# A four-layer graph network on one core: who evicts the first attention layer's products, and who sums the second layer's rows

## What is computed

```python
def _gat_conv(x, W, att_src, att_dst, b, src, dst):
    h = (x @ W).reshape(n, HEADS, HID)                     # 4 heads of 64
    a_s = jnp.einsum('nhc,hc->nh', h, att_src)
    a_d = jnp.einsum('nhc,hc->nh', h, att_dst)
    e = jax.nn.leaky_relu(a_s[src] + a_d[dst], NEG_SLOPE)
    m = jax.ops.segment_max(e, dst, num_segments=n)
    ex = jnp.exp(e - m[dst])
    denom = jax.ops.segment_sum(ex, dst, num_segments=n)
    alpha = ex / denom[dst]
    msg = h[src] * alpha[:, :, None]
    return jax.ops.segment_sum(msg, dst, num_segments=n).reshape(n, HEADS * HID) + b
...
h = jax.nn.elu(_gat_conv(x, W1, att_src1, att_dst1, b1, src, dst))   # src, dst with self-loops
h = jax.nn.elu(_gat_conv(h, W2, att_src2, att_dst2, b2, src, dst))
...
x = _layernorm(x + h)
```

## Time and profile before

| | us |
|---|---|
| median of 3 runs | 7264.87 (7262.79 to 7265.74) |
| the profiled execution | 7259.0 |
| its span | 7257.3 |
| first attention layer, 2860 to 3552 of the span | 692 |
| second attention layer, 3552 to 4400 | 848 |
| graph convolution layer, 4400 to 4872 | 472 |
| third attention layer, 5533 to 6330 | 797 |
| last attention layer, 6330 to 7257 | 927 |

### The profile page before, as it was taken

How to read it: one execution, slowest core, us unless ns; L and a number is a source line. 1 busy time by engine, 2 the same in 40 slices (tenths; PEclk the granted TensorE clock), 3 DMA queues, 4 the chain that set the end, 5 groups by cost and what they waited for, 6 DMA issues and landing times. The chain is left out here.

```text
span 7257.3 us, 77301 instructions
## 1 busy us (share of the span) xinstructions
PE 3818.6 (53%) x18205; PEld 3002.3 (41%) x18205; DVE 4910.7 (68%) x15616; ACT 3204.3 (44%) x7082; POOL 3988.0 (55%) x3216
## 2 busy tenths in 40 slices
PE   3578880088866884777400005988884666700000
PEld 1267760077755663555400003547773555600000
DVE  6544555545548875999698886866666888676664
ACT  0023330033324552444255555758884777633333
POOL 4767776667766877342244425621114444178887
PEclk9689995599998997999755557999997888855555
DMA  8745447845448996676577767989995666476665
GB/s 307 273 92 77 77 64 272 328 69 78 77 56 318 350 348 212 234 245 235 186 260 260 249 244 286 380 302 327 334 336 188 215 219 211 163 265 226 226 227 188
DMA packets 646102, 1633.93 MB, mean 225 GB/s; under 512 B 128454, under 2 KB 283878, under 8 KB 630290
## 3 DMA queue, kind: packets, MB, share of 16 engines
q1 hardware_dynamic: 459954, 1234.83, 48.9%
q0 software_dynamic: 185696, 394.18, 20.3%
HBM read 816.50 MB, written 813.62 MB: 225 GB/s over the span
## 5 line engine op out<-in xcount | busy, mean ns | idle before, releaser
L1708 PE MATMUL l_pb<-l_jx,k_ones 128*128 128x128 f32 x26 | 6.1, 399 | 1595.9 <-DVE l_jx L1941 1595.9
L802 POOL DMA_INDIRECT NS<-e_tot,e_idx x392 | 647.9, 1653 | 283.3 <-ACT e_tot L1060 210.8
L2244 ACT ACTIVATE l_z<-l_a,l_nb,l_rs 128x256 f32<-128x256 f32 x1176 | 609.7, 598 | 392.7 <-DMA out_dram<-l_z,k_ids 389.9
L1667 POOL DMA_INDIRECT l_eg<-HBT,k_nsrc x392 | 508.2, 1296 | 384.8 <-DVEq L1886 145.0
L1708 PEld LDWEIGHTS l_pb<-l_jx,k_ones 128*128 128x128 f32 x26 | 5.0, 284 | 1596.6 <-DVE l_jx L1941 1596.6
L936 DVE TENSOR_SCALAR e_eq<-e_pk,z_skey 128x128 f32<-128x128 f32 x588 | 204.1, 347 | 621.7 <-DMA NS<-e_tot,e_idx 590.4
L2131 POOL TENSOR_TENSOR l_rs<-l_ve,k_minus_half 128x8 f32<-128x8 f32 x147 | 259.7, 1767 | 533.9 <-DVE l_ve L2414 241.3
L2166 PE MATMUL l_pm<-k_w_L3b,l_zt 128*128 128x258 f32 x1568 | 406.8, 419 | 218.8 <-ACT l_o L2214 214.5
L2138 POOL DMA_INDIRECT out_dram<-l_z,k_ids x392 | 422.1, 1077 | 119.5 <-issue 109.0
L1203 POOL DMA_INDIRECT XH<-n_o,z_home x392 | 399.7, 1020 | 119.2 <-issue 112.4
L2279 ACT ACTIVATE l_a<-l_a,l_eshare 128x64 f32<-128x64 f32 (+1 forms) x1372 | 378.9, 360 | 186.2 <-DVE l_eshare L1923 144.0
(11 more groups left out here) (384 smaller groups left out, 13063.6 us busy)
## 6 DMA issues: line engine op xcount, KB each, us to landing
NS<-z_zero SPq DMA_DIRECT2D x200, 520.0 KB
HBT<-l_o SPq DMA_DIRECT2D x196, 528.0 KB
l_a<-HBT SPq DMA_DIRECT2D x196, 528.0 KB, 9.2
GSUMS<-l_erun SPq DMA_DIRECT2D x72, 1056.0 KB, 5.0
l_a<-XH SPq DMA_DIRECT2D x98, 528.0 KB
HA<-n_o SPq DMA_DIRECT2D x98, 528.0 KB, 7.9
l_a<-HA SPq DMA_DIRECT2D x98, 528.0 KB
n_r<-NS SPq DMA_DIRECT2D x98, 520.0 KB
```

The source lines that it names most:

```text
L802: pool.indirect_dma_start(out=nodes, out_offset=bass.IndirectOffsetOnAxis(ap=idx[q % DEEP][:, k:k + 1], axis=0), in_=tot[q % 2][:, k, :], ...
L1667: pool.indirect_dma_start(out=self.g[b % self.ng][:, k, :], out_offset=None, in_=self.table, in_offset=bass.IndirectOffsetOnAxis(ap=self.i ...
L2244: last = act.activation(z[:, j, 0:D], a[:, j, 0:D], ACT.Identity, bias=self.nb[b][:, col:col + 1], scale=self.rs[b][:, col:col + 1])
```

## The change

Three things, in the two attention stages of the second layer:

1. In the first stage ScalarE evicts the products, by plain copies, and nothing is added to them. The constant `row_b` is therefore missing from the rows of HBT and from the logits.
2. In the second stage the logits get their constant at the head: `logit_b` (zeros for the source half, the sum of both constants for the target half) is added to all of `asd` before anything reads it.
3. In the second stage the row that the elu takes is summed by TensorE in PSUM (`ps`, two buffers of two banks): the own rows times the identity, for region 0 also `part` times the identity, and `row_b` times a row of ones. ScalarE scales all four groups of own rows (`self_act` 4), VectorE only forms `part`, and both halves of the elu read PSUM.

```diff
@@ setup_phase, VectorE @@
                 dve.tensor_tensor(S["row_b"][:], S["row_b"][:], carry[0][:, 0:RW], ALU.subtract)
+                dve.memset(S["logit_b"][:], 0.0)
+                dve.drain()
+                dve.tensor_tensor(S["logit_b"][:, HEADS:2 * HEADS], S["row_b"][:, D:D + HEADS], S["row_b"][:, D + HEADS:RW], ALU.add)
@@ Edges.tensor, tick 0 @@
+            if self.bias is not None:
+                pe.wait_ge(self.s_ad, 1)
@@ Edges.target_logits @@
+        if self.bias is not None:
+            lk.link(dve.tensor_tensor(S["asd"][:], S["asd"][:], over_columns(self.bias[:], C), ALU.add))
+            lk.settle(dve)
+            dve.sem_inc(self.s_ad, 1)
@@ Nodes.tensor @@
+        now = self.tile(tick, "pre") if self.summed else None
+        if now:
+            u, region, t = now
+            ps, a = self.ps[u % 2], self.a[u % self.ra]
+            if u >= 2:
+                pe.wait_ge(self.s_elu, u - 1)
+            pe.wait_ge(self.s_in[u % self.ra], self.loaded(u))
+            if region == 0:
+                pe.wait_ge(self.s_sum, t + 1)
+                pe.wait_ge(self.s_self, t + 1)
+            for h in range(2):
+                js = slice(h * (J // 2), (h + 1) * (J // 2))
+                pe.matmul(ps[:, js, :], S["ident"][:], a[:, js, 0:D], start=True, stop=False)
+                if region == 0:
+                    pe.matmul(ps[:, js, :], S["ident"][:], self.part[t % 2][:, js, :], start=False, stop=False)
+                last = pe.matmul(ps[:, js, :], S["ones"][0:1, :], over_columns(S["row_b"][0:1, 0:D], J // 2), start=False, stop=True)
+            last.then_inc(self.s_ps, 1)
@@ Nodes.scalar @@
-        now = self.tile(tick, "evict") if self.mat and kind != "l1a" else None
+        now = self.tile(tick, "evict") if self.mat else None
...
-                        act.activation(S["asd"][:, J * t + h * (J // 2):J * t + (h + 1) * (J // 2), 0:2],
-                                       self.pm[h][:, :, D:D + 2], ACT.Copy)
+                        act.activation(S["asd"][:, J * t + h * (J // 2):J * t + (h + 1) * (J // 2), 0:self.wc - D],
+                                       self.pm[h][:, :, D:self.wc], ACT.Copy)
...
-                if region == 0:
+                if self.summed:
+                    act.wait_ge(self.s_ps, u + 1)
+                elif region == 0:
                     act.wait_ge(self.s_sum, t + 1)
...
-                act.activation(self.ee[u % 2][:], a[:, :, 0:D], ACT.Exp, bias=S["minus_one"][:]).then_inc(self.s_ee, 1)
+                v = self.ps[u % 2][:] if self.summed else a[:, :, 0:D]
+                act.activation(self.ee[u % 2][:], v, ACT.Exp, bias=S["minus_one"][:]).then_inc(self.s_ee, 1)
@@ Nodes.vector @@
-        now = self.tile(tick, "evict") if self.kind == "l1a" else None
-        if now:
-            parts.append(self.evict(dve, *now))
@@ Nodes.sum_up @@
             part = self.part[t % 2]
+            if self.summed:
+                dve.wait_ge(self.s_self, t + 1)
+                if t >= 2:
+                    dve.wait_ge(self.s_ps, self.place[t - 2] + 1)
+                dve.tensor_tensor(by_head(part[:]), by_head(run), spread(sh[:, 1, k0:k0 + J, :], hw), ALU.mult).then_inc(self.s_sum, 1)
+                return
@@ Nodes.body @@
-            elu = dve.scalar_tensor_tensor(a[:, :, 0:D], self.ee[u % 2][:], 1.0, a[:, :, 0:D], ALU.min, ALU.max)
+            v = self.ps[u % 2][:] if self.summed else a[:, :, 0:D]
+            elu = dve.scalar_tensor_tensor(a[:, :, 0:D], self.ee[u % 2][:], 1.0, v, ALU.min, ALU.max)
@@ gnn_kernel @@
-        layer_phase(nc, S, "l2", dict(kind="l1b", rows=T["HBT"], rw=RW, resid=x1, out=T["X2"], self_act=2),
-                    dict(table=T["HBT"], tw=RW, index=S["nsrc32"], acc=T["GSUMS"]))
+        layer_phase(nc, S, "l2", dict(kind="l1b", rows=T["HBT"], rw=RW, resid=x1, out=T["X2"], self_act=4),
+                    dict(table=T["HBT"], tw=RW, index=S["nsrc32"], acc=T["GSUMS"], bias=S["logit_b"]))
```

More of the change, by code:

```diff
@@ L1571, with __init__ @@
 class Edges:
-    def __init__(self, nc, S, s, table, tw, index, acc, heads, first, load=None):
+    def __init__(self, nc, S, s, table, tw, index, acc, heads, first, load=None, bias=None):
+        self.bias, self.s_ad = bias, s.sem("target_logits_biased")
         self.S, self.table, self.tw, self.index, self.heads, self.load, self.acc = S, table, tw, index, heads, load, acc
@@ L2030, in __init__ @@
             self.s_dd = s.sem("squares_ready")
+        self.summed = kind == "l1b"
+        if self.summed:
+            self.ps = [s.ps(f"ps{b}", [P, J, D]) for b in range(2)]
+            self.s_ps = s.sem("rows_summed")
+            self.s_elu = s.sem("elu_ready")
         if self.elu:
@@ L2067, in __init__ @@
                 self.wc = RW if kind == "l1a" else D + 2
+    place = SPOT
     def ticks(self):
@@ L2143, in tensor @@
     def tensor(self, pe, tick):
+        S = self.S
+        now = self.tile(tick, "pre") if self.summed else None
[15 more added lines that the diff above has]
+            last.then_inc(self.s_ps, 1)
         if not self.mat:
             return
-        S = self.S
         now = self.tile(tick, "prod")
@@ L2255, in scalar @@
                 if u >= 2:
-                    act.wait_ge(self.s_u, u - 1)
-                act.activation(self.ee[u % 2][:], a[:, :, 0:D], ACT.Exp, bias=S["minus_one"][:]).then_inc(self.s_ee, 1)
+                    act.wait_ge(self.s_elu if self.summed else self.s_u, u - 1)
+                v = self.ps[u % 2][:] if self.summed else a[:, :, 0:D]
+                act.activation(self.ee[u % 2][:], v, ACT.Exp, bias=S["minus_one"][:]).then_inc(self.s_ee, 1)
         u = tick - self.L["pre"] + 1
@@ L2376, in body @@
                 return
-            lk.link(elu)
+            elu.then_inc(self.s_elu, 1)
             yield
-            lk.settle(dve)
+            dve.wait_ge(self.s_elu, u + 1)
             r = self.r[u % self.rr]
@@ L2422, in shifts @@
         yield
-    def evict(self, dve, u, region, t):
-        S, o, b = self.S, self.o[u % self.ro], u % self.ro
-        if u >= self.ro:
-            dve.wait_ge(self.s_os[b], 16 * (u // self.ro))
-        for h in range(2):
-            dve.wait_ge(self.s_m, 2 * u + h + 1)
-            js = slice(h * (J // 2), (h + 1) * (J // 2))
-            if region == 0:
-                dve.tensor_tensor(S["asd"][:, J * t + h * (J // 2):J * t + (h + 1) * (J // 2), :], self.pm[h][:, :, D:RW],
-                                  over_columns(S["row_b"][:, D:RW], J // 2), ALU.add)
-            dve.tensor_tensor(o[:, js, :], self.pm[h][:, :, 0:RW], over_columns(S["row_b"][:], J // 2), ALU.add).then_inc(self.s_o, 1)
-            yield
     def add_neighbours(self, dve, u, region, t):
@@ L2536, in gnn_kernel @@
             ("bnscale", [P, KC], F32), ("bnshift", [P, KC], F32), ("w_L2", [P, KC, D], F32),
-            ("row_b", [P, RW], F32),
+            ("row_b", [P, RW], F32), ("logit_b", [P, 2 * HEADS], F32),
         ):
```

## The result

The changed kernel takes 7329.21 us (median of 4 runs, 7323.58 to 7334.89) against 7265.31 before: ratio 1.0085, with a 95% interval of 1.0064 to 1.0105. It is 64 us slower; the forecast was 7247, and its range ended at 7295. The profiled execution took 7331.41 us, span 7329.6. (Of the four executions of e13, a run described further down, one took 14103.97 us, twice the others; its ratio leaves that one out.)

The account below looks back on a forecast made before the run. VectorE was taken as the fullest engine in both attention layers, until a wait replaces its work. Terms -23 + 3 + 2 + 1 = -17, stated as -18 us, gave 7247 us against 7264.87, range 7170 to 7295.

Parts of the forecast that it names:

- The busy times and the forms of waiting: Both attention layers: VectorE busy near 470 and 660 us, ScalarE near 446 and 522, with longer or new waits on ScalarE.
- the elu from PSUM at no extra: Second layer: VectorE's elu reading PSUM instead of SBUF was to cost 0 us extra.
- They start when the run part is there and are wanted a tick (8 us) later: Second layer: TensorE's added products, 0.86 us each, were to be hidden at full and three-quarter clock, costing nothing.
- rival 3: Second layer: TensorE at its lower clock bounds the stage, 842 us at 1.2 GHz; some +40, 7300 us; chance 0.05.
- the 421: Second layer: TensorE's time for the added products at full clock, 49 x 8.6 = 421 us.
- the own-row wait: Second layer: VectorE waits for ScalarE's own rows ahead of the run part, about 88 us; bounds 0 to 142.
- The forecast's 85 us off VectorE: Second layer: VectorE loses the own-row product and the run part's addition, 10.4 us a cycle, 85 over the stage.
- +3: Second layer: waits of 10.8 us a cycle against 10.4 saved, over eight cycles, +3 us.
- -23 forecast: First layer: eviction moved to ScalarE saves 3.2 us a cycle over 7.3 cycles, -23 us.
- Waits 18.0 instead of 6.6, work 14.6 less: First layer, per 11-tick cycle: VectorE's waits grow and its work shrinks, a net gain of 3.2 us.
- my lower bound: First layer: gain of 0 us if ScalarE's part is 3 us a cycle longer than in the walk.
- The upper bound, 106: First layer: 130 x 80/98 = 106 us less if every new wait is covered.

Follow-up runs that it names:

- e13: e6 with ScalarE doing the exponential first in its tick in both attention layers; ratio 0.9751 to the kernel before the change.
- e1: Changed kernel with the constant's one-row product replaced by one of 128 rows (identity); ratio 1.0013 to the kernel before, second layer 867.8 us.
- a0: The changed kernel run once more, unedited, on the chip of the experiments; ratio 1.0077 to the kernel before, second layer 918.3 us.
- e9: Changed kernel with the constant's product given 32 rows of 1/32; ratio 1.0085 to the kernel before, second layer 917.1 us.
- e3: Changed kernel with the first layer put back as before and no constant or logit bias, leaving the second layer's PSUM sum; ratio 1.0016 to the kernel before.
- e2: Changed kernel with the constant's products left out of the second layer; ratio 1.0004 to the kernel before, second layer 863.1 us.
- e4: Kernel before with only the first layer changed (ScalarE evicts plain copies, constant left out); ratio 0.9982 to the kernel before, first layer 688.5 us.
- e6: Changed kernel with the 128-row identity constant and no wait of VectorE for the own rows; ratio 0.9883 to the kernel before, second layer 782.7 us.

## Why the prediction was wrong, step by step

**The busy times and the forms of waiting: right.** VectorE, ScalarE, the new wait of the run part, the exponential ahead of which the copies stand, and the elu from PSUM at no extra. On the last, the estimate from the Trainium skill (VectorE: DVE Perf Modes, the table in "The TRN2 errata") was some 6 us more for 98 elus. The trace has 1213 against 1214 ns, and decides.

**Second layer, the step that failed: "They start when the run part is there and are wanted a tick (8 us) later ...: hidden at full clock, and at three quarters of it too."** The product's price of 0.86 us was read from a stretch of 128-row products at full clock and used for all 490. But 196 of the 490 have one row. With them a product took 1.05 us at full clock, and for much of the layer the array stood at 1.2 GHz, at 2.00 us a product. The term that I had at 0 measured 50 us in the layer: e1 against a0. That was rival 3, at "some +40, 7300" and a chance of 0.05. What I held against it, that TensorE would be "busy without a pause, and so wouldn't stay there", is what the 50.00 of 50 us at 0.51 refute; the pause at the start of a tile, which I held for it, is not what made the 50 us, since e1 has the pauses and 0.81. The 842 us that rival 3 took for the whole layer at 1.2 GHz were twice the 421; by the 2.00 us measured, 490 products make 980, an estimate, more than the layer has. The Trainium skill (TensorE: Matmul & The Clock Gate, "Part 1: The HAM clock gate") has the clock come back under sustained work. The stretches without a pause agree where all products have 128 rows (e1), and don't where every other one has one row (0.51) or 32 (0.55). In its section on "Why this matters for your kernels" the same page of the Trainium skill says that a product of 32 rows takes the same time as one of 128. In e9 the products take 1.05 us at full clock, against 0.86 in e1, and 2.00 near the end: here the measurement differs.

**Second layer, the own-row wait: right in size, incomplete in worth.** 88 forecast, 103.5 measured (94.9 in e1), and its removal gives 85 to 86. The forecast's 85 us off VectorE are 80 (745 to 665). Without one-row products the layer came to +17 (e1, with the 4.8 us of the head), where I had +3, and +2 for the bias. The parts are +9 for the sum in PSUM (e3), +3 for the bias (e2 against e3, with the head), and +5 for the constant's products even with 128 rows (e1 against e2), which I had at nothing. So 12 us were missing beside the 50.

**First layer, a term mis-sized: -23 forecast, -9 to -10 measured** (e4, changed kernel). "Waits 18.0 instead of 6.6, work 14.6 less" a cycle (by its own terms the work is 14.7): the wait for the exponential grew to 162 us over the stage instead of 120 to 150. Between the heads of the two stages VectorE has 128 us less work (601 to 473) and 116 more of this wait. My walk lacked ScalarE's wait for TensorE between the halves, 39.8 us in all, and the lower clock behind TensorE's longer waits for ScalarE. The result lies about midway between the forecast and my lower bound ("0 if ScalarE's part is 3 us a cycle longer"). The upper bound, 106, was no idle one: 70 came under another order.

**The sum.** -23 + 3 + 2 + 1 = -17 became -10 + 17 + 50 = +57 by stages, +64 by the medians; the rest lies in stages that nothing touches, within their spread from trace to trace.

## What to carry to other kernels

Before a product that adds a constant goes on an idle TensorE, look at its rows: with one row each for 196 of its 490 products, the stage had a mean clock of 0.64, and a 128-row stationary (here the identity, on a constant that all partitions hold) gave 50 us, and 151 with the exponential first. Ask of every wait whether the engine touches what it waits for: one that it doesn't need cost 85 us, and all that the change took off VectorE in that layer was 80. And where work is moved to an engine, look at what others wait for in its order: with the exponential first the same move was worth 70 us instead of 9. But first in order pays only if it is ready: with the one-row products late, the same order cost 71 us.

## What was not expected of the hardware

With 50.00 of 50 us busy TensorE stayed at a granted clock of 0.51 while every other product had one row, and went at 0.86 us a product in the same place with 128. The clock also fell from 1.00 without any pause before it, and at 1.00 the alternation cost 1.05 us a product against 0.86; whether that has the same cause is open. With 32 rows the granted clock lies between (0.70) and the time is the same as with one; which tiles that helps, and why none that set the time, stays open, as does any number of rows between 32 and 128. Two costs that I took for alternatives, the low clock and the wait for own rows, added up in full (50 and 86 us, 136 between a0 and e6).
